# First attention: the triangular mask moves from TensorE's score sums to a selection by GpSimd on the exponentials

## The chip, the cores and the metric

The kernel runs on one core of one Trainium2 chip. The metric is the device time of the whole program in microseconds (us), lower is better. The kernel before takes 4102.77 us (median of three runs, 4102.47 to 4106.52).

## The reference, cut to what matters

Two transformer blocks run one after the other on x of shape 4 x 2048 x 256: an attention, a layer norm, a feed-forward part and a layer norm, twice. Both attentions have 16 heads of dimension 16 and are causal. The change is in the first one, whose score is a sum of three terms:

```python
scores = alpha * tanh(q @ k.T / beta)                 # per head
scores = scores + lam * hamming + lat                 # low-rank terms from x @ hex_w.T and x @ q6_w.T
scores = where(tril, scores, -inf)                    # keys after the query drop out
attn   = softmax(scores, axis=-1)
out    = attn @ v
```

Only the square blocks on the diagonal of the score matrix hold pairs on both sides of the triangle; blocks past it are never computed.

## The kernel before, in words

The program is a list of phases, one after the other: setup, projection of the first batch element, first attention (`attend_phase` with layer 0), a middle phase, second attention (layer 1), and a last phase. The change touches `attend_phase`, layer 0 only. The second attention masks in another way (VectorE takes the minimum with a table, `diagonal`) and is not altered.

**Tiling.** Scores are held transposed, keys on the 128 partitions and queries along the free axis. One *set* is one batch element and four heads; there are 16 sets. A set is a list of 34 *steps* (`even_steps`), 544 steps in all, each 128 partitions x (4 heads x 512 columns). The columns of a step are one key block against 512 queries, or two pieces of other widths. Ten steps of a set touch the diagonal. Steps 0, 7, 17 and 32 have one diagonal block of 128 columns for each head (512 elements per partition over the four heads); steps 1, 3, 8, 18, 20 and 33 have two (1024 elements per partition). Over 16 sets that is 64 and 96 steps.

**What each engine does for step S.** The engines run their own loops over S, tied by counting semaphores:

- TensorE, in iteration S of its loop and in this order: `weigh(S-2)` (probabilities of step S-2 times v, so LAG is 2), `extra(S,0)`, `extra(S,1)` (the low-rank score terms of heads 0 and 1), some background pieces, `scores(S+1, ...)` (q times k for the four heads of the next step, which waits for tanh of step S to have read its banks), `extra(S,2)`, more pieces, `extra(S,3)`. Each `extra` waits until VectorE has read the bank of two heads before.
- ScalarE alternates: tanh of step S (L929), then exp of step S-1 in place in `prob` (L940).
- VectorE, in `sums`, makes for each head alpha x tanh + extra into `prob` (L1004, four instructions of 128 x 512). Before the third of them it does one part of the normalisation of a finished group of queries, where one is due: a transpose (L971), a reciprocal (L974), a product (L978) or a transpose (L982).
- `prob` has R = 4 buffers; `sums(S)` waits for `weigh(S-4)`.

**The mask before.** In `extra`, for a piece on the diagonal, a second matmul (L866) adds a 128 x 128 table with -1e30 above the triangle to the bank. exp then gives zero there. `weigh(S)` waits for the count `pr`, that is, for exp of step S.

**Background.** While the first three batch elements are attended, the projections of the next one are made in the gaps: `pieces_at` on TensorE, `evict` on VectorE, and on GpSimd the split of each projected tile in three bf16 parts (L1033 to L1040, four instructions each for seven tiles per unit of 512 rows). This happens in sets 0 to 11; sets 12 to 15 have none, and there GpSimd has nothing at all to do. The plan gives pieces to TensorE in steps 9, 12 to 16, 19 and 24 to 31 of a set.

**Order.** SyncE issues loads three query groups ahead, stores of projected tiles and stores of results; all wait on counts of other engines. GpSimd issues no transfer.

Of the kernel before, what the change touches and what calls it, by code (L numbers as in the profile page):

```python
# [21 lines left out]
ALU = mybir.AluOpType  # L22
# [4 lines left out]
P = 128  # L27
# [5 lines left out]
CB = TG // P  # L33
HQ = 4
# [577 lines left out]
def attend_phase(nc, kn, layer, w=None):  # L612
# [7 lines left out]
    kept_at = [sum(1 for _, m in steps[:s] if m) for s in range(NST)]  # L620
    N_SET = B * NHQ
    N = N_SET * NST
    NG = N_SET * GB
    ND = sum(1 for _, m in steps if m)
    R = 4
    LAG = 2
    QU, KU = 3, 6
    QK0, E0, O0 = 0, 4, 6
# [3 lines left out]
    NU = len(kinds)  # L632
    NX = (B - 1) * GB if layer == 0 else 0
# [26 lines left out]
    with ExitStack() as ctx:  # L660
# [6 lines left out]
        sc = ph.count("sc")  # L667
        pr = ph.count("pr")
        kept = ph.count("kept")
        pv = ph.count("pv")  # L670
        o_tr, o_rc, o_mul, o_n = (ph.count(n) for n in ("o_tr", "o_rc", "o_mul", "o_n"))
# [5 lines left out]
        if layer == 0:  # L677
            f_s = ph.sb("f", [FR, QU, HQ, TG], BF16)
            g_s = ph.sb("g", [FR, KU, TG], BF16)
            tanh_s = ph.sb("tanh", [P, 2, HQ, TG])  # L680
        prob = ph.sb("prob", [P, R, HQ, TG])
# [4 lines left out]
        if layer == 0:  # L686
            w_in, x_in, ones_set = ph.sem("w_in"), [ph.sem(f"x_in{u}") for u in range(2)], ph.sem("ones_set")
            bg_ps, bg_ev = ph.count("bg_ps"), ph.count("bg_ev")
            hi, rest, mid, low = (ph.count(n) for n in ("hi", "rest", "mid", "low"))
# [9 lines left out]
        ps = kn["ps"]  # L699
        N_LOAD = NPART * (4 if layer == 0 else 2) + 2  # L700
        block = ctx.enter_context(nc.Block())

        def at(S):

            it, s = divmod(S, NST)
            return (it, s) + steps[s]
# [96 lines left out]
        def _(pe):  # L803
# [52 lines left out]
                    qk.done(mm)  # L856

            def extra(S, h):
                it, _, pieces, masked = at(S)

                sc.wait(pe, S * HQ + h - 2)
                for g, kb, q0, col, w in pieces:
                    n, c = it * GB + g, it * GB + kb // CB
                    mm = pe.matmul(ps[:, E0 + h % 2, col:col + w], g_s[:, c % KU, (kb % CB) * P:(kb % CB + 1) * P], f_s[:, n % QU, h, q0:q0 + w], start=True, stop=not masked)  # L864
                    if masked:
                        mm = pe.matmul(ps[:, E0 + h % 2, col:col + P], kn["identb"][:], kn["mask_kq"][:], start=False, stop=True)  # L866
                ex.done(mm)

            def weigh(S):
                it, s, pieces, masked = at(S)  # L870
                if layer == 0:
                    pr.wait(pe, S)
                elif masked:
                    kept.wait(pe, (it * ND + kept_at[s]) * 2 + 1)
                else:
                    pr.wait(pe, S * 2 + 1)
                for g, kb, q0, col, w in pieces:
                    n, c = it * GB + g, it * GB + kb // CB
                    if kb == 0:

                        o_tr.wait(pe, n - 2)
                        X = it - 1 if g == 0 else it
                        if g in ahead and 0 <= X < NX:

                            bg_ev.wait(pe, X * NU + ahead[g])
                    for h in range(HQ):
                        mm = pe.matmul(ps[VW * h:VW * (h + 1), O0 + n % 2, q0:q0 + w], v_s[:, c % KU, kb % CB, h * VW:(h + 1) * VW], prob[:, S % R, h, col:col + w], start=kb == 0, stop=g in ends[s] and (g, kb) == [p[:2] for p in pieces if p[0] == g][-1])  # L887
                pv.done(mm)
# [52 lines left out]

        @block.vector
        def _(dve):
            for c in (sc, o_tr, o_rc, o_mul, o_n, kept) + ((bg_ev,) if layer == 0 else ()):
                c.start(dve)
            dve.memset(oq_s[:], 0.0).then_inc(padded, 1)
            dve.wait_ge(padded, 1)
            if layer == 0:
                dve.memset(vs[:], 1.0).then_inc(ones_set, 1)
                dve.wait_ge(ones_set, 1)  # L950

            def evict(j):

                X, kind, m, tile, n, bank = unit(j)
                if kind == "v":
                    bg_ps.wait(dve, j)
                    v_out.wait(dve, m, X - 1)
                    bg_ev.done(dve.tensor_copy(vs[:, m, :, :, 0:HD], ps[:, bank].rearrange("p (t h d) -> p t h d", t=2, h=H)))
                elif kind != "g":
                    bg_ps.wait(dve, j)  # L960
                    low.wait(dve, tile - 2)
                    bg_ev.done(dve.tensor_copy(raw[0:n, tile % 2], ps[0:n, bank]))  # L962

            def normalise(due, count):

                for S, G, part in due[:count]:
                    v = G % 2
                    if part == 0:
                        pv.wait(dve, S)
                        o_mul.wait(dve, G - 2)  # L970
                        o_tr.done(dve.transpose(ot_s[:, v].rearrange("p b n -> p (b n)"), ps[:, O0 + v]))  # L971
                    elif part == 1:
                        o_tr.wait(dve, G)
                        o_rc.done(dve.reciprocal(rc_s[:, v], ot_s[:, v, :, HD]))  # L974
                    elif part == 2:
                        o_rc.wait(dve, G)
                        o_n.wait(dve, G - 2)
                        o_mul.done(dve.tensor_tensor(oq_s[:, v, :, 0:HD], ot_s[:, v, :, 0:HD], rc_s[:, v].unsqueeze(2).to_broadcast([P, NTB, HD]), ALU.mult))  # L978
                    else:
                        o_mul.wait(dve, G)  # L980
                        o_out.wait(dve, v, G // 2 - 1)
                        o_n.done(dve.transpose(on_s[:, v], oq_s[:, v].rearrange("p b n -> p (b n)")))  # L982
                del due[:count]

            def diagonal(S):

                masked = at(S)[3]
                for pair in range(2):
                    pr.wait(dve, S * 2 + pair)
                    block = blocks(prob[:, S % R, 2 * pair:2 * pair + 2], masked)  # L990
                    kept.done(dve.tensor_tensor(block, block, kn["keep"][:].unsqueeze(1).unsqueeze(1).to_broadcast([P, 2, len(masked), P]), ALU.min))  # L991

            def sums(S, due):

                pv.wait(dve, S - R)
                for h in range(HQ):
                    if h == 0 and unit_at(S) is not None:
                        evict(unit_at(S))
                    if h == 2:

                        normalise(due, 1)
                    th.wait(dve, S)
                    ex.wait(dve, S * HQ + h)
                    sc.done(dve.scalar_tensor_tensor(prob[:, S % R, h], tanh_s[:, S % 2, h], kn["alpha"][:, 0:1],  # L1004
                                                     ps[:, E0 + h % 2], ALU.mult, ALU.add))

            due = []
            for S in range(N + LAG + 1):
                if S > LAG:
                    it, s, *_ = at(S - LAG - 1)  # L1010
                    due += [(S - LAG - 1, it * GB + g, part) for g in ends[s] for part in range(4)]
                if S < N and layer == 0:
                    sums(S, due)
                else:
                    if S < N and at(S)[3]:
                        diagonal(S)
                    normalise(due, len(due))
            assert not due

        if layer == 0:  # L1020
            @block.gpsimd
            def _(pool):
                for c in (hi, rest, mid, low):
                    c.start(pool)
                for j in range(NX * NU):
                    X, kind, m, tile, n, bank = unit(j)
                    if kind == "v":
                        continue
                    u = tile % 2
                    src = f12[:, X % 2] if kind == "g" else raw[0:n, u]  # L1030
                    bg_ev.wait(pool, j)
                    parts_out.wait(pool, u, tile // 2 - 1)
                    hi.done(pool.tensor_copy(parts[0:n, u, 0], src))  # L1033
                    hi.wait(pool, tile)
                    low.wait(pool, tile - 1)
                    rest.done(pool.tensor_tensor(rem[0:n], src, parts[0:n, u, 0], ALU.subtract))
                    rest.wait(pool, tile)
                    mid.done(pool.tensor_copy(parts[0:n, u, 1], rem[0:n]))  # L1038
                    mid.wait(pool, tile)
                    low.done(pool.tensor_tensor(parts[0:n, u, 2], rem[0:n], parts[0:n, u, 1], ALU.subtract))  # L1040


def row_max_phase(nc, kn, layer, w=None):
# [990 lines left out]
```

## Time and profile before

| | |
|---|---|
| median of the runs | 4102.77 us |
| the profiled execution | 4100.62 us |
| its span, first to last instruction | 4098.8 us |
| mean granted TensorE clock | 0.97 |
| busy: TensorE / VectorE / ScalarE / GpSimd | 3696.2 / 2527.2 / 3502.5 / 623.6 us |
| first attention, first tanh to the end of the last exp | 133.5 to 2287.7 us |

Busy time says how long an engine had an instruction in work. Matmuls are pipelined, so that a busy TensorE is not one at its peak: the distance between the starts of successive instructions says what one of them costs, not its duration. Successive ScalarE instructions overlap by about 0.1 us in the same way.

### The profile page before, as it was taken

The numbers are of one execution on the slowest core, as the hardware profiler recorded it, in microseconds if no ns is written. First come the engines' busy times: TensorE is split into PE (matmuls) and PEld (weight loads), VectorE is DVE, ScalarE is ACT, GpSimd is POOL, SyncE is SP. The second block draws the span as 40 slices with busy tenths as digits, with TensorE's granted clock in tenths as the row PEclk, the third lists the DMA queues.
The fourth block names the chain that finished last, engine by engine and source line by source line (L and its number), as shares of the span: only waits on it lengthen the run. The fifth ranks groups of instructions, "written<-read, shape, count | busy, mean of one in ns | idle before, by whom it ended". The sixth has DMA issues, their size and how long they took to land. (4 is left out here: it accounts for less than half of the span.)

```text
span 4098.8 us, 62490 instructions
## 1 busy us (share of the span) xinstructions
PE 3696.2 (90%) x22198; PEld 1474.5 (36%) x22198; DVE 2527.2 (62%) x4349; ACT 3502.5 (85%) x2970; POOL 623.6 (15%) x659
## 2 busy tenths in 40 slices
PE   5699999999999999999989699969999999999798
PEld 2233333333333333333223366622222222222575
DVE  5577877787778777877788566732232323232576
ACT  2598999998999998999999566659999999999466
POOL 3112121211121112110000055510000000000232
PEclk9799999999999999999999899979999999999899
DMA  4322232222222322221121277642222222221331
GB/s 149 116 72 71 68 87 67 78 66 85 66 75 68 87 69 73 60 85 42 38 60 33 98 191 194 156 110 67 75 72 75 75 74 71 71 78 44 115 93 52
DMA packets 274745, 340.51 MB, mean 83 GB/s; under 512 B 40142, under 2 KB 207918, under 8 KB 274161
## 3 DMA queue, kind: packets, MB, share of 16 engines
q1 hardware_dynamic: 274420, 336.38, 28.1%
q8 instruction: 179, 2.93, 0.3%
q14 instruction: 146, 1.20, 0.1%
HBM read 207.97 MB, written 128.25 MB: 82 GB/s over the span
## 5 line engine op out<-in xcount | busy, mean ns | idle before, releaser
L1004 DVE SCALAR_TENSOR_TENSOR att_prob<-att_tanh,alpha,ps 128x512 f32<-128x512 f32 x2176 | 1513.9, 741 | 348.1 <-ACT att_tanh L929 189.7
L854 PE MATMUL ps<-att_q,att_k 99*128 99x512 bf16 (+5 forms) x5120 | 1138.5, 351 | 84.0 <-DMA att_v<-v_ones 61.2
L887 PE MATMUL ps<-att_prob,att_v 128*32 128x512 f32 (+3 forms) x10240 | 1173.3, 544 | 1.9 <-ACT att_prob L940 1.9
L929 ACT ACTIVATE att_tanh<-ps,rbeta 128x2048 f32<-128x2048 f32 x544 | 1083.4, 1992 | 73.6 <-PE ps L854 63.7
L940 ACT ACTIVATE att_prob<-att_prob 128x2048 f32<-128x2048 f32 x544 | 1053.2, 1936 | 91.7 <-DVE att_prob L1004 90.7
L935 ACT ACTIVATE att_prob<-ps 128x1024 f32<-128x1024 f32 x1088 | 1054.3, 1021 | 25.9 <-PE ps L854 9.8
L864 PE MATMUL ps<-att_f,att_g 75*128 75x512 bf16 (+3 forms) x2560 | 815.2, 357 | 159.4 <-DVE att_prob L1004 148.6
L854 PEld LDWEIGHTS ps<-att_q,att_k 96*128 96x128 bf16 (+1 forms) x5120 | 415.3, 98 | 897.2 <-ACT att_prob L935 427.3
L864 PEld LDWEIGHTS ps<-att_f,att_g 75*128 75x128 bf16 x2560 | 228.8, 97 | 942.9 <-DVE att_prob L1004 908.4
L991 DVE TENSOR_TENSOR att_prob<-att_prob,keep 128x512 f32<-128x512 f32 (+1 forms) x320 | 187.5, 586 | 580.6 <-ACT att_prob L935 579.5
L887 PEld LDWEIGHTS ps<-att_prob,att_v 128*32 128x32 f32 x10240 | 216.8, 108 | 367.1 <-issue 148.4
L1912 POOL TENSOR_SCALAR post_prev<-post_xt,post_om 128x512 f32<-128x512 f32 x64 | 56.8, 905 | 1233.0 <-issue 1124.6
L866 PE MATMUL ps<-mask_kq,identb 128*128 128x128 bf16 x1024 | 212.5, 221 | 0.0
L971 DVE STREAM_TRANSPOSE att_ot<-ps 128x512 f32<-128x512 f32 x128 | 91.2, 712 | 180.3 <-PE ps L887 180.3
L1683 POOL TENSOR_TENSOR mid_x1b<-mid_x,mid_bias 128x256 f32<-128x256 f32 x64 | 44.5, 729 | 626.2 <-ACT mid_x L1282 626.2
L1033 POOL CAST att_parts<-att_raw 128x512 bf16<-128x512 f32 (+1 forms) x72 | 43.8, 609 | 580.3 <-DVE att_raw L962 537.3
L1282 ACT ACTIVATE post_x<-post_rr,post_n_nb,post_n_rs 128x256 f32<-128x256 f32 x128 | 66.4, 589 | 65.6 <-DVE post_n_nb L1271 65.6
L1033 POOL CAST att_parts<-att_f 12x512 bf16<-12x512 f32 x12 | 7.2, 599 | 731.2 <-ACT att_f L922 731.2
L962 DVE COPY att_raw<-ps 128x512 f32<-128x512 f32 (+1 forms) x72 | 49.7, 690 | 98.0 <-PE ps L832 44.5
L1494 ACT ACTIVATE mid_parts<-mid_qcos 128x512 bf16<-128x512 f32 x64 | 40.1, 626 | 81.8 <-POOL mid_qcos L1657 81.6
L866 PEld LDWEIGHTS ps<-mask_kq,identb 128*128 128x128 bf16 x1024 | 101.2, 99 | 2.6 <-issue 0.7
L1040 POOL TENSOR_TENSOR att_parts<-att_rem,att_parts 128x512 bf16<-128x512 f32 (+2 forms) x84 | 97.1, 1156 | 15.1 <-POOL att_parts L1038 15.1
(162 smaller groups left out, 2975.7 us busy)
## 6 DMA issues: line engine op xcount, KB each, us to landing
att_v<-v_ones SPq DMA_DIRECT2D x128, 256.0 KB
att_k<-k_parts SPq DMA_DIRECT2D x128, 192.0 KB
att_q<-q_parts SPq DMA_DIRECT2D x128, 192.0 KB
att_k<-k_parts SPq DMA_DIRECT2D x128, 128.0 KB
att_q<-q_parts SPq DMA_DIRECT2D x128, 128.0 KB
o_t<-att_on SPq DMA_DIRECT2D x512, 32.0 KB, 1.8
v_ones<-mid_vs SPq DMA_DIRECT2D x64, 256.0 KB, 3.3
v_ones<-att_vs SPq DMA_DIRECT2D x96, 128.0 KB, 2.1
```

Source lines behind the costliest of these rows:

```text
L854: mm = pe.matmul(ps[:, bank, col:col + w], keys, q_s[:, n % QU, h, q0:q0 + w], start=True, stop=True)
L864: mm = pe.matmul(ps[:, E0 + h % 2, col:col + w], g_s[:, c % KU, (kb % CB) * P:(kb % CB + 1) * P], f_s[:, n % QU, h, q0:q0 + w], start=True ...
L866: mm = pe.matmul(ps[:, E0 + h % 2, col:col + P], kn["identb"][:], kn["mask_kq"][:], start=False, stop=True)
L887: mm = pe.matmul(ps[VW * h:VW * (h + 1), O0 + n % 2, q0:q0 + w], v_s[:, c % KU, kb % CB, h * VW:(h + 1) * VW], prob[:, S % R, h, col:col + ...
L929: th.done(act.activation(tanh_s[:, S % 2], ps[:, QK0:QK0 + HQ], ACT.Tanh, scale=kn["rbeta"][:, 0:1]))
L935: pr.done(act.activation(prob[:, S % R, 2 * pair:2 * pair + 2], ps[:, bank:bank + 2], ACT.Exp, scale=float(HD) ** -0.5))
L940: pr.done(act.activation(prob[:, (S - 1) % R], prob[:, (S - 1) % R], ACT.Exp))
L971: o_tr.done(dve.transpose(ot_s[:, v].rearrange("p b n -> p (b n)"), ps[:, O0 + v]))
L991: kept.done(dve.tensor_tensor(block, block, kn["keep"][:].unsqueeze(1).unsqueeze(1).to_broadcast([P, 2, len(masked), P]), ALU.min))
L1004: sc.done(dve.scalar_tensor_tensor(prob[:, S % R, h], tanh_s[:, S % 2, h], kn["alpha"][:, 0:1], ps[:, E0 + h % 2], ALU.mult, ALU.add))
L1040: low.done(pool.tensor_tensor(parts[0:n, u, 2], rem[0:n], parts[0:n, u, 1], ALU.subtract))
L1282: ins = act.activation(dst(t), src(t), ACT.Identity, scale=self.rs[:, u, t:t + 1], bias=self.nb[:, u, t:t + 1])
```

## The change

`extra` no longer issues the table's matmul (L866). Masked elements therefore go through tanh, sum and exp like all the others. On GpSimd a new function `hide(S)` waits for exp of step S (`pr`), and one `affine_select` in place writes zero where the key lies after the query, over the four heads and the one or two diagonal blocks of the step. It counts `kept`. `weigh(S)` of a masked step waits for `kept` in place of `pr`; the others wait for `pr` as before. GpSimd's loop now runs over the steps, with `hide(S-1)` ahead of the split of a tile that was finished in step S-1.

```diff
             def extra(S, h):
...
-                    mm = pe.matmul(ps[:, E0 + h % 2, col:col + w], g_s[...], f_s[...], start=True, stop=not masked)
-                    if masked:
-                        mm = pe.matmul(ps[:, E0 + h % 2, col:col + P], kn["identb"][:], kn["mask_kq"][:], start=False, stop=True)
+                    mm = pe.matmul(ps[:, E0 + h % 2, col:col + w], g_s[...], f_s[...], start=True, stop=True)
             def weigh(S):
                 it, s, pieces, masked = at(S)
-                if layer == 0:
+                if masked and layer == 0:
+                    kept.wait(pe, it * ND + kept_at[s])
+                elif layer == 0:
                     pr.wait(pe, S)
...
+                zero = pool.to_reg(0.0)
+                def hide(S):
+                    pr.wait(pool, S)
+                    block = blocks(prob[:, S % R], at(S)[3])
+                    kept.done(pool.affine_select(block, block, [[0, HQ], [0, len(at(S)[3])], [1, P]], ALU.is_ge, zero, base=0, channel_multiplier=-1))
...
+                for S in range(N + 1):
+                    if S > 0 and at(S - 1)[3]:
+                        hide(S - 1)
+                    if S > 0 and unit_at(S - 1) is not None:
+                        split(unit_at(S - 1))
```

## Rows read from the trace of the kernel before

**Rows 1.** Busy time by engine in two stretches: the first attention, set 12.

```profile
133.00:2288.00 2155.00, 1966.16 (x11974) 717.92 (x11976) 1688.59 (x2524) 2021.14 (x1100) 296.47 (x336) 0.98 0.23 68
...
1787.00:1911.00 124.00, 112.17 (x706) 36.25 (x704) 99.83 (x153) 124.00 (x69) 0.00 (x0) 1.00 0.17 51
```

**Rows 2.** Timeline, one plain iteration (set 14, step 16): start, duration, engine, line.

```profile
2092.45 2.01 ACT L940 ACTIVATE att_prob<-att_prob 128x2048 f32<-128x2048 f32 x1
...
2094.26 2.06 ACT L929 ACTIVATE att_tanh<-ps,rbeta 128x2048 f32<-128x2048 f32 x1
2094.54 0.16 PEld L887 LDWEIGHTS ps<-att_prob,att_v 128*32 128x32 f32 x8 [0.23 <-ACT att_prob L940]
...
2095.54 0.61 PE L864 MATMUL ps<-att_f,att_g 75*128 75x512 bf16 x2
...
2096.38 1.04 PE L854 MATMUL ps<-att_q,att_k 96*128 96x512 bf16 x4 [0.24 <-ACT att_tanh L929]
2096.41 2.73 DVE L1004 SCALAR_TENSOR_TENSOR att_prob<-att_tanh,alpha,ps 128x512 f32<-128x512 f32 x4 [0.92 <-ACT att_tanh L929]
...
2097.91 2.07 ACT L929 ACTIVATE att_tanh<-ps,rbeta 128x2048 f32<-128x2048 f32 x1
...
2099.76 2.02 ACT L940 ACTIVATE att_prob<-att_prob 128x2048 f32<-128x2048 f32 x1
```

**Rows 3.** Timeline of ScalarE, set 4: steps 20 and 32 and their successors.

```profile
765.41 1.97 ACT L929 ACTIVATE att_tanh<-ps,rbeta 128x2048 f32<-128x2048 f32 x1
...
769.48 1.95 ACT L929 ACTIVATE att_tanh<-ps,rbeta 128x2048 f32<-128x2048 f32 x1
...
815.26 1.97 ACT L929 ACTIVATE att_tanh<-ps,rbeta 128x2048 f32<-128x2048 f32 x1
...
819.63 1.95 ACT L929 ACTIVATE att_tanh<-ps,rbeta 128x2048 f32<-128x2048 f32 x1
```

**Rows 4.** Groups of instructions: the mask's matmuls (busy, mean ns | idle).

```profile
L866 PE MATMUL ps<-mask_kq,identb 128*128 128x128 bf16 x1024 | 212.5, 221 | 0.0
```

**Rows 5.** Timeline of TensorE in set 4: one of them, and its successor.

```profile
767.98 0.22 PE L866 MATMUL ps<-mask_kq,identb 128*128 128x128 bf16 x1
768.04 0.27 PE L864 MATMUL ps<-att_f,att_g 75*128 75x256 bf16 x1
```

**Rows 6.** Groups of instructions on GpSimd, in three phases (busy, mean ns | idle).

```profile
L1657 POOL TENSOR_TENSOR mid_qcos<-mid_qcos,mid_qsin 128x512 f32<-128x512 f32 x64 | 80.8, 1274 | 108.5 <-DVE mid_qsin L1583 108.3 <-issue 0.2
...
L1912 POOL TENSOR_SCALAR post_prev<-post_xt,post_om 128x512 f32<-128x512 f32 x64 | 56.8, 905 | 1233.0 <-issue 1124.6 <-ACT post_xt L1839 108.4
...
L1033 POOL CAST att_parts<-att_raw 128x512 bf16<-128x512 f32 (+1 forms) x72 | 43.8, 609 | 580.3 <-DVE att_raw L962 537.3 <-DMA k_parts<-att_parts 43.1
```

**Rows 7.** Timeline: ScalarE hands over to GpSimd, and GpSimd to ScalarE.

```profile
453.42 0.57 ACT L922 ACTIVATE att_f<-ps 12x512 f32<-12x512 f32 x1
...
454.25 0.60 POOL L1033 CAST att_parts<-att_f 12x512 bf16<-12x512 f32 x1 [60.67 <-ACT att_f L922]
...
2439.87 0.63 ACT L1494 ACTIVATE mid_parts<-mid_qcos 128x512 bf16<-128x512 f32 x1 [0.17 <-POOL mid_qcos L1657]
```

**Rows 8.** Timeline, an iteration with a transpose (set 13, step 14).

```profile
1964.76 1.41 DVE L1004 SCALAR_TENSOR_TENSOR att_prob<-att_tanh,alpha,ps 128x512 f32<-128x512 f32 x2 [0.60 <-ACT att_tanh L929]
...
1966.09 0.70 DVE L982 STREAM_TRANSPOSE att_on<-att_oq 128x512 f32<-128x512 f32 x1
...
1966.71 1.36 DVE L1004 SCALAR_TENSOR_TENSOR att_prob<-att_tanh,alpha,ps 128x512 f32<-128x512 f32 x2
...
1968.11 2.02 ACT L940 ACTIVATE att_prob<-att_prob 128x2048 f32<-128x2048 f32 x1
```

**Rows 9.** The product L978: its durations (minimum/median/maximum ns), and one beside GpSimd.

```profile
L978 DVE TENSOR_TENSOR att_oq<-att_ot,att_rc x128: 416/424/1362, 173.7 to 3798.4; 128x256 f32<-128x256 f32 x128
...
468.05 1.16 POOL L1036 TENSOR_TENSOR att_rem<-att_raw,att_parts 128x512 f32<-128x512 f32 x1 [0.28 <-POOL att_parts L1033]
...
468.13 1.36 DVE L978 TENSOR_TENSOR att_oq<-att_ot,att_rc 128x256 f32<-128x256 f32 x1
```

More of the change, by code:

```diff
@@ L858, in extra @@
             def extra(S, h):
-                it, _, pieces, masked = at(S)
+                it, _, pieces, _ = at(S)
                 sc.wait(pe, S * HQ + h - 2)
@@ L863, in extra @@
                     n, c = it * GB + g, it * GB + kb // CB
-                    mm = pe.matmul(ps[:, E0 + h % 2, col:col + w], g_s[:, c % KU, (kb % CB) * P:(kb % CB + 1) * P], f_s[:, n % QU, h, q0:q0 + w], start=True, stop=not masked)
-                    if masked:
-                        mm = pe.matmul(ps[:, E0 + h % 2, col:col + P], kn["identb"][:], kn["mask_kq"][:], start=False, stop=True)
+                    mm = pe.matmul(ps[:, E0 + h % 2, col:col + w], g_s[:, c % KU, (kb % CB) * P:(kb % CB + 1) * P], f_s[:, n % QU, h, q0:q0 + w], start=True, stop=True)
                 ex.done(mm)
@@ L943, in _ @@
         def _(dve):
-            for c in (sc, o_tr, o_rc, o_mul, o_n, kept) + ((bg_ev,) if layer == 0 else ()):
+            for c in (sc, o_tr, o_rc, o_mul, o_n) + ((bg_ev,) if layer == 0 else (kept,)):
                 c.start(dve)
@@ L1022, in _, with split @@
             def _(pool):
-                for c in (hi, rest, mid, low):
+                for c in (hi, rest, mid, low, kept):
                     c.start(pool)
-                for j in range(NX * NU):
+                zero = pool.to_reg(0.0)
[3 more added lines that the diff above has]
+                    kept.done(pool.affine_select(block, block, [[0, HQ], [0, len(at(S)[3])], [1, P]], ALU.is_ge, zero, base=0, channel_multiplier=-1))
+                def split(j):
                     X, kind, m, tile, n, bank = unit(j)
                     if kind == "v":
-                        continue
+                        return
                     u = tile % 2
```

## The prediction

> **What bounds the kernel now.** I read the busy time by stretch first. In the first attention (2155 us) ScalarE is busy 2021 us, TensorE 1966; in set 12, where no projections run beside it, ScalarE is busy 124.00 of 124.00 us and GpSimd does nothing [rows 1]. So the stage runs at ScalarE's pace. The timeline then gives the period: tanh starts at 2094.26 and again at 2097.91, so a step costs 3.65 us (tanh plus exp) [rows 2]. 544 steps x 3.65 = 1986 us; the rest of the stage is steps in which something reaches ScalarE late. The question is what is late after the change, and by how much; TensorE's busy share says nothing here.
>
> I put the plain iteration on a clock that starts with tanh(S) at 0 [rows 2]: exp(S-2) ends at 2094.46, that is 0.20; weigh(S-2) starts at 0.28; the first two extras start at 1.28; scores(S+1) run from 2.12 (they wait for the end of tanh(S)) to 3.16; tanh(S+1) starts at 3.65. VectorE's four sums run from 2.15 to 4.88, exp(S) starts at 5.50. weigh(S-2) starts 0.08 after the exp that it needs: it has no spare time of its own, only what lies behind it on TensorE has.
>
> **What goes.** 1024 mask matmuls, 212.5 us of busy time [rows 4]. But the next matmul starts 0.06 us after the mask's [rows 5], so what TensorE gets back is 1024 x 0.06 = 61 us, and only where TensorE is what ScalarE waits for is it worth anything. In set 4 two masked steps are longer than 3.65: step 20 (765.41 to 769.48, 4.07) and step 32 (815.26 to 819.63, 4.37) [rows 3]. In the 12 sets with projections this is at most 12 x (0.42 + 0.72) = 14 us; both have background pieces around them. Up to four masks stand ahead of the scores (0.24 us); step 20 is followed by a select's wait anyway, so I count 2 us.
>
> **What comes.** 160 selections, 64 of 512 and 96 of 1024 elements per partition, each between exp(S-2) and weigh(S-2). The trace has no selection. GpSimd's one-input rows for 512 elements take 0.61 us (cast) and 0.905 us (two constants, f32 to f32); two inputs take 1.274 us [rows 6]. Lower bound: 1024 elements at the price of a 1.5-fold cast, D = 0.9 (D1 = 0.6 for 512); upper: twice the two-input row, D = 2.55 (D1 = 1.27). The nearest row is the two-constant one, as a selection also computes a value, compares and writes f32: D1 = 0.9 and twice that, D = 1.8. Handing over costs too: ScalarE's instruction ends at 453.99 and GpSimd's starts at 454.25, 0.26 us; out of GpSimd 0.17 us are seen towards ScalarE [rows 7], 0.15 towards TensorE is my estimate. So weigh(S-2) starts at w = 0.20 + 0.26 + D + 0.15 = D + 0.61 in place of 0.28.
>
> The Trainium skill (GPSIMD Engine Reference, section 3.1) gives about 1.8 cycles per element at best for a tight loop at 1.2 GHz, 0.77 us for 512 elements; estimated from that page D would be 1.54 and, by the sum below, the time about 4203 us. The 0.905 us row of this trace is slower than that rule.
>
> **What is late then.** Queued behind weigh on TensorE are the extras, the scores and the last extras; ScalarE waits for the scores, VectorE for the extras, ScalarE for VectorE. Without masks the scores start 1.0 + 0.44 after w at the earliest and end at w + 2.48; with 0.04 to hand over, tanh(S+1) is late by w + 2.52 - 3.65 = **D - 0.52**. VectorE's first sum follows the first extra by 0.53 (estimate: 0.39 us matmul and a handover), ends at w + 1.53 + 2.73, so exp(S) is late by w + 4.30 - 5.50 = D - 0.59: less. But with a normalising transpose before the third sum VectorE takes 3.31 us (1964.76 to 1968.07) and exp follows after 0.04, at 5.50: no spare time there [rows 8]. Then exp(S) is late by w + 4.88 - 5.50 = **D**. With a reciprocal (0.25) it is D - 0.3.
>
> The iterations that wait for a selection are S = M + 2 for masked step M. A transpose is due in iterations 2, 5 and 9 of a set (groups of queries end in steps 3, 8, 20 and 33, the four parts fall due from three steps later), that is for M = 0, 3 and 7; a reciprocal in iteration 3, for M = 1. Two masked steps in a row share: the second exp is done on time while tanh was held, so the second selection starts early by what the first one cost, and the pair costs what the second alone would, or the first if more. Per set, with D = 1.8:
> - M = 3: D = 1.80
> - M = 7, 8: larger of D1 = 0.9 and D - 0.52 = 1.28
> - M = 17, 18: 1.28; M = 20: 1.28; M = 32, 33: 1.28
> - M = 0, 1 (next set): D - 0.3 = 1.50
>
> Sum 8.42 us, or 6D - 2.4; x 16 sets = 135 us. In the 12 sets with projections TensorE is late for other reasons in some of these iterations (step 20 by 0.42 [rows 3]), and a selection hides behind that; I take twice that, 0.84 us per set, 10 us, off. Take off 2 us for the masks, add 2 for the last selection, with nothing behind it. **+125 us.**
>
> Other edits cost nothing: GpSimd's splits run in the same order, and a split takes four instructions of 0.6 to 1.2 us within a step or so of its eviction; each masked step after one is over a step away. GpSimd issues no transfer, and no queue is passed. The second attention is untouched.
>
> The profiled execution took 4100.62 us (span 4098.8), 2.15 less than the median; 4100.6 + 125 = 4225.6, and beside the median **4228 us**.
>
> **The rivals.**
> - *The selection is longer than any GpSimd row suggests*, D over 2.55. For: it computes an index per element, and no row does. Against: all 512-element rows lie between 0.6 and 1.3. At D = 2.55 the sum is 16 x 12.9 = 206, less 10: 4299 us. At D = 3.5, 16 x 18.6 - 10 = 288: 4391 us.
> - *VectorE's product and the selection block each other.* L978 takes 0.42 us, but 1.36 beside a GpSimd instruction that ends at 469.21; it ends at 469.49 [rows 9]: it waited for it. The sums do not show this, and the product is due in iterations 4, 8, 13 and 25, about 3.5 after tanh, while selections start 0.46 after tanh in iteration M + 2. In iterations 4 and 8 (next to M = 3 and 7) they miss each other by some 0.1 us. If they meet: up to 2 per set x 16 x 1.4 us (1.8 less 0.4 spare) = 45 us: 4273 us. The Trainium skill (SBUF — State Buffer, SBUF: two separate sides) calls the shared pair of ports an exclusive lock, held for a whole instruction, for a VectorE instruction with two SBUF inputs. The trace agrees, with this row.
> - *Not slower*: the selection fits in what TensorE has spare, and the masks' 14 us come back. Place: the wait of weigh. It decides at D = 0.52 for plain iterations, while M = 3, 7 and 0 cost D or D1 whatever it is; with D = 0.2 and D1 = 0.1 it is 16 x 0.4 = 6 us against up to 14: 4103 - 8 = 4095 us. Against: no row for 512 elements is under 0.6 us.
> - *The spare time is larger than I read*, the lower bound of D with pairs fully shared: D = 0.9, 16 x 3.3 - 10 = 43 us: 4146 us. This is the low edge of the forecast, not another mechanism.
>
> **How the numbers follow.** Forecast with D from 0.9 to 2.55: 0.80. Longer selection: 0.10. Blocking with VectorE: 0.05. Not slower: 0.05, of which 0.02 is faster by over 0.2% (8 us, about what a measurement can tell from no change) and 0.03 within. Slower: 0.95. The range takes the forecast's own bounds, 4146 and 4299, and a little of the longer selection: 4145 to 4310 us.
>
> **What would show it.** The L866 group is gone; a GpSimd group of 160 selections stands at about 0.9 us (64) and 1.8 us (96). The wait of weigh's weight loads on GpSimd is 160 times some 2 us. Tanh starts in iterations 2, 5 and 9 to 10, 19 to 20, 22, 0 to 1 and 3 come 3.65 plus the stalls above; all others keep 3.65; the second attention keeps its length. ScalarE stays at 3.65 us of work per step and is idle some 125 us more. I am wrong in size if the selection is not 1.8 us, in mechanism if it is and the stalls per set are not 6D - 2.4, or if steps that wait for no selection become longer.

## The result, and the profile after

The changed kernel takes 4171.0 us (median of four runs, 4166.9 to 4179.2) against 4103.9 us: ratio 1.0168, 95% interval 1.0156 to 1.0180, 67 us slower. It was forecast slower, 4228 us with a range of 4145 to 4310: the direction and the main mechanism hold, the amount is about half of the 125 us forecast.

The profiled execution took 4169.7 us, 69.1 more than that of before. From the first tanh of the first attention to the last, it is 2216.5 us and was 2147.2: all 69 us are in this stage. First the busy time by engine, in the whole stage and in set 13 (no projections); they answer to [rows 1]. Each such row has the stretch and its length, the busy time (and count of instructions) of TensorE, its weight loads, VectorE, ScalarE and GpSimd, then the granted clock as a share of 2.4 GHz, the DMA share and GB/s.

```profile
133.00:2357.00 2224.00, 1925.25 (x10943) 660.94 (x10940) 1680.35 (x2524) 2035.40 (x1100) 443.76 (x495) 0.97 0.22 66
1967.90:2095.80 127.90, 107.68 (x642) 32.96 (x641) 100.61 (x154) 126.44 (x70) 9.98 (x11) 1.00 0.17 50
```

ScalarE is no longer busy all the time in a set without projections (126.44 of 127.90). Then the selection, by group and by its spread (minimum/median/maximum ns), and who waited for it. The mask's matmuls [rows 4] are gone.

```profile
L1032 POOL TENSOR_SCALAR_AFFINE_SELECT att_prob<-att_prob 128x1024 f32<-128x1024 f32 (+1 forms) x160 | 148.8, 930 | 1327.0 <-ACT att_prob L940 1294.2
...
L1032 POOL TENSOR_SCALAR_AFFINE_SELECT att_prob<-att_prob x160: 652/1098/1111, 141.9 to 2357.4; 128x1024 f32<-128x1024 f32 x96, 128x512 f32<-128x512 f32 x64
...
PEld ps L887 <- POOL att_prob L1032: 137.8, 134, 3.2
PE ps L887 <- POOL att_prob L1032: 99.3, 116, 2.3
```

The timeline of iteration 3 of set 13, which waits for the selection of step 1 (two blocks); it answers to [rows 2]. As in the prediction, w is the start of weigh, counted from the start of that iteration's tanh.

```profile
1977.40 1.90 ACT L940 ACTIVATE att_prob<-att_prob 128x2048 f32<-128x2048 f32 x1
1979.20 1.96 ACT L929 ACTIVATE att_tanh<-ps,rbeta 128x2048 f32<-128x2048 f32 x1
1979.46 1.10 POOL L1032 TENSOR_SCALAR_AFFINE_SELECT att_prob<-att_prob 128x1024 f32<-128x1024 f32 x1 [3.27 <-ACT att_prob L940]
1980.62 0.38 PEld L887 LDWEIGHTS ps<-att_prob,att_v 128*32 128x32 f32 x16 [1.20 <-POOL att_prob L1032]
...
1981.62 0.61 PE L864 MATMUL ps<-att_f,att_g 75*128 75x256 bf16 x4
...
1982.07 1.03 PE L854 MATMUL ps<-att_q,att_k 96*128 96x512 bf16 x4
...
1983.14 1.97 ACT L929 ACTIVATE att_tanh<-ps,rbeta 128x2048 f32<-128x2048 f32 x1
```

exp ends at 1979.30, the selection starts 0.16 later, takes 1.10 and ends at 1980.56, weigh follows 0.06 later: w is 1.42. The scores end at 1983.10, and the next tanh comes 3.94 after the last in place of 3.65. The forecast's relation w + 2.52 - 3.65 gives 0.29, and 0.29 it is. With one block (here iteration 9 of set 14) the selection takes 0.68 us and w is 1.00:

```profile
2130.66 1.96 ACT L929 ACTIVATE att_tanh<-ps,rbeta 128x2048 f32<-128x2048 f32 x1
...
2130.93 0.68 POOL L1032 TENSOR_SCALAR_AFFINE_SELECT att_prob<-att_prob 128x512 f32<-128x512 f32 x1 [14.32 <-ACT att_prob L940]
2131.66 0.16 PEld L887 LDWEIGHTS ps<-att_prob,att_v 128*32 128x32 f32 x8 [1.03 <-POOL att_prob L1032]
```

Iteration 5 of set 13, with a normalising transpose on VectorE; it answers to [rows 8].

```profile
1986.81 1.95 ACT L929 ACTIVATE att_tanh<-ps,rbeta 128x2048 f32<-128x2048 f32 x1
...
1989.75 1.41 DVE L1004 SCALAR_TENSOR_TENSOR att_prob<-att_tanh,alpha,ps 128x512 f32<-128x512 f32 x2 [1.23 <-PE ps L864]
...
1991.07 0.71 DVE L982 STREAM_TRANSPOSE att_on<-att_oq 128x512 f32<-128x512 f32 x1
...
1993.10 1.91 ACT L940 ACTIVATE att_prob<-att_prob 128x2048 f32<-128x2048 f32 x1 [0.40 <-DVE att_prob L1004]
```

exp starts 6.29 after tanh, not 5.50: late by 0.79; w + 4.88 - 5.50 gives 0.80.

I took the starts of all 544 tanh from both timelines and compared them step by step. Regular differences, the same in nearly every set (us per set):

```
iteration    waits for        by the forecast's formula   measured, sets
             selection of     at w = 1.42 or 1.00         with projections / without
1            33 (32 before)   0.29                        0.28 / 0.34
3            1  (0 before)    0.50 (reciprocal)           0.28 / 0.24
5 and 6      3                0.80 (transpose)            0.80 / 0.79
9 and 10     7, 8             0.38 (transpose)            0.65 / 0.38
19 and 20    17, 18           0.29                        0.58 / 0.32
22           20               0.29                        0.28 / 0.28
24           none (cause open) -                          0.18 / 0.13
sum                           2.55                        3.05 / 2.5
```

Iteration 2 waits for a selection too (step 0) and has a normalising transpose, but is no later than before (0.02): iteration 1 just ahead of it had already been held.

12 x 3.05 + 4 x 2.5 = 47 us. Beside them stand 12 iterations, in steps 3, 9, 19 and 22 of some sets, that are another 1.5 to 2.1 us longer, some 19 us in all. The last 4 us are spread over other steps. One of the 12 (set 14, step 3), and the granted clock over it and over its sibling in set 13 (the column behind POOL's):

```profile
2106.33 1.10 POOL L1032 TENSOR_SCALAR_AFFINE_SELECT att_prob<-att_prob 128x1024 f32<-128x1024 f32 x1 [3.27 <-ACT att_prob L940]
...
2107.48 1.93 PE L887 MATMUL ps<-att_prob,att_v 128*32 128x128 f32 x16 [0.90 <-POOL att_prob L1032]
...
2109.35 1.03 PE L864 MATMUL ps<-att_f,att_g 75*128 75x256 bf16 x4
...
2111.59 1.97 ACT L929 ACTIVATE att_tanh<-ps,rbeta 128x2048 f32<-128x2048 f32 x1 [1.60 <-PE ps L854]
...
2106.00:2112.00 6.00, 4.91 (x33) 2.11 (x37) 3.73 (x8) 4.34 (x4) 1.10 (x1) 0.72 0.38 117
1979.00:1985.00 6.00, 4.56 (x39) 1.63 (x38) 4.99 (x9) 5.93 (x4) 1.10 (x1) 1.00 0.42 133
```

The selection and weigh's start are the same as in set 13; then weigh takes 1.93 us and not 1.07. The granted clock is 1.00 (2.4 GHz) from 2106.07 to 2107.40, while TensorE waits, and 0.50 (1.2 GHz) from 2107.50 to 2110.80, from weigh's start on; over the 6 us that is 0.72. Set 13 has the same wait and keeps its clock. In all 12 the clock falls between 0.9 and 1.9 us after tanh, about where weigh starts (1.00 or 1.42).

### The profile page after: what moved, and what is told of

Its sections match the earlier page's. It is cut to its first block and busy times, and to the rows that moved or that the text cites. A ratio compares the mean times of both kernels' runs of the same rounds, so it can differ in the third digit from the quotient of the medians.

```text
span 4167.9 us, 60763 instructions
## 1 busy us (share of the span) xinstructions
PE 3654.7 (88%) x21174; PEld 1418.7 (34%) x21174; DVE 2517.8 (60%) x4349; ACT 3516.7 (84%) x2970; POOL 771.8 (19%) x819
## 5 line engine op out<-in xcount | busy, mean ns | idle before, releaser
L929 ACT ACTIVATE att_tanh<-ps,rbeta 128x2048 f32<-128x2048 f32 x544 | 1068.3, 1964 | 115.2 <-PE ps L854 106.8
L940 ACT ACTIVATE att_prob<-att_prob 128x2048 f32<-128x2048 f32 x544 | 1038.0, 1908 | 104.5 <-DVE att_prob L1004 100.7
L864 PE MATMUL ps<-att_f,att_g 75*128 75x512 bf16 (+3 forms) x2560 | 785.4, 361 | 171.2 <-DVE att_prob L1004 170.5
L854 PEld LDWEIGHTS ps<-att_q,att_k 96*128 96x128 bf16 (+1 forms) x5120 | 428.2, 98 | 894.7 <-ACT att_prob L935 425.9
L864 PEld LDWEIGHTS ps<-att_f,att_g 75*128 75x128 bf16 x2560 | 201.9, 97 | 957.0 <-DVE att_prob L1004 883.0
L1032 POOL TENSOR_SCALAR_AFFINE_SELECT att_prob<-att_prob 128x1024 f32<-128x1024 f32 (+1 forms) x160 | 148.8, 930 | 1327.0 <-ACT att_prob L940 1294.2
L1673 POOL TENSOR_TENSOR mid_qcos<-mid_qcos,mid_qsin 128x512 f32<-128x512 f32 x64 | 80.8, 1274 | 108.6 <-DVE mid_qsin L1599 108.4
L1050 POOL TENSOR_TENSOR att_parts<-att_rem,att_parts 128x512 bf16<-128x512 f32 (+2 forms) x84 | 97.1, 1156 | 15.1 <-POOL att_parts L1048 15.1
L982 DVE STREAM_TRANSPOSE att_on<-att_oq 128x512 f32<-128x512 f32 x128 | 90.6, 707 | 2.2
L1598 DVE TENSOR_TENSOR mid_qcos<-ps,mid_cos 128x512 f32<-128x512 f32 x64 | 44.0, 687 | 72.6 <-PE ps L1436 71.5
```

The costliest lines, as they stand in the source:

```text
L854: mm = pe.matmul(ps[:, bank, col:col + w], keys, q_s[:, n % QU, h, q0:q0 + w], start=True, stop=True)
L929: th.done(act.activation(tanh_s[:, S % 2], ps[:, QK0:QK0 + HQ], ACT.Tanh, scale=kn["rbeta"][:, 0:1]))
L940: pr.done(act.activation(prob[:, (S - 1) % R], prob[:, (S - 1) % R], ACT.Exp))
L1032: kept.done(pool.affine_select(block, block, [[0, HQ], [0, len(at(S)[3])], [1, P]], ALU.is_ge, zero, base=0, channel_multiplier=-1))
```

## The experiments

Two questions: is the wait the whole loss, and where do the iterations at the lower clock come from? No mask, aside, both masks (first time) and later ran together on one chip (kernel before there: 4102.9 us), twice, fill, between and LAG 3 on a second (4102.9), and the changed kernel again, both masks again and the last two LAG 3 kernels on a third (4103.5). Each ratio is to the kernel before on the same chip. The edits are against the changed kernel unless it says otherwise.

**No mask.** In `weigh` and GpSimd's loop:

```diff
-                if masked and layer == 0:
-                    kept.wait(pe, it * ND + kept_at[s])
-                elif layer == 0:
+                if layer == 0:
                     pr.wait(pe, S)
...
-                    if S > 0 and at(S - 1)[3]:
-                        hide(S - 1)
```

> Leaves out the triangular mask of the first attention altogether: no mask matmuls, no selection, weigh waits for exp. Theory (the selection's latency ahead of weigh is the whole loss, and the masks' matmuls were hidden behind ScalarE): before minus 0 to 5 us, some 4100 us. Rival (the matmuls taken away were worth what stands before them in steps 20 and 32, 14 us, so that the selection cost 80 and not 67 us): 4090 us.

Measured: 4101.3 us against 4102.9, ratio 0.9996 (0.9987 to 1.0005). Against before only step 20 changed regularly: 0.24 us or more shorter in the sets with projections, 4 us in all; step 32 kept its 4.36. So 212 us of busy matmuls were worth at most some 4 us in the profile, and no more than the noise in the medians (1.6 us, the interval holds 1); the selection with its wait costs about 70 and not 80.

**Selection aside.**

```diff
+            scr_s = ph.sb("scr", [P, HQ, 2, P])
...
+                if layer == 0:                  # weigh
                     pr.wait(pe, S)
...
+                if S >= R and at(S - R)[3]:     # sums
+                    kept.wait(dve, o_it * ND + kept_at[o_s])
...
+                    kept.wait(pool, it * ND + kept_at[s] - 1)
-                    kept.done(pool.affine_select(block, block, ...))
+                    kept.done(pool.affine_select(scr_s[:, :, 0:len(at(S)[3])], block, ...))
```

> The 160 selections are made, but into a scratch tile that nobody reads; weigh waits for exp only, so the mask is left out of the result. VectorE waits for the selection of four steps earlier before it overwrites what was read, which has long ended. Theory (only the wait costs): the same as without any mask, within 3 us, some 4100 us. Rival (GpSimd's reads of SBUF hold up VectorE or its own splits): 4115 us or more, with L978 or L1043 late.

Measured: 4101.8 us, ratio 0.9995 (0.9986 to 1.0004), the same as without any mask. The selections are all there and as long as before:

```profile
L1036 POOL TENSOR_SCALAR_AFFINE_SELECT att_scr<-att_prob x160: 651/1098/1109, 141.7 to 2289.5; 128x1024 f32<-128x1024 f32 x96, 128x512 f32<-128x512 f32 x64
```

GpSimd's work, its traffic in SBUF and its place ahead of the splits cost nothing that these medians show; only that weigh waits for it does. This rules out the rival in which the selection and VectorE's product block each other: of the 128 products L978, 22 take some 1.36 us in the changed kernel, 24 in this one, and 23 did before, beside GpSimd's splits [rows 9].

**Both masks**, run twice.

```diff
-                    ... start=True, stop=True)
+                    ... start=True, stop=not masked)
+                    if masked:
+                        mm = pe.matmul(ps[:, E0 + h % 2, col:col + P], kn["identb"][:], kn["mask_kq"][:], start=False, stop=True)
```

> The mask matmuls are put back, the selection and its wait stay. Theory: where TensorE is late because of the selection, in iterations 1, 3 and 20 of a set, the up to four mask matmuls ahead of the scores (0.06 us each) now stand on the path: 3 x 0.24 x 16 = 11 us more than the changed kernel, some 4182 us. Rival (the masks' matmuls keep TensorE busier and its clock up, so that the slow stretches go): 4155 us.

> Selection and mask matmuls together once more, on the same chip as the changed kernel. Theory (the mask matmuls cost 6 to 11 us on the path in iterations 1, 3 and 20, and take away slow stretches of TensorE in iterations 9, 19 and 22 by keeping it busy in the masked steps ahead): 8 to 18 us less than the changed kernel on the same chip. Rival (the 15 us between them were the chance of two chips): the same, or up to 11 us more.

Measured: 4156.0 us (four runs, ratio 1.0124) the first time, 4165.1 (4152.8 to 4168.0, ratio 1.0143) the second. The changed kernel beside the second:

> The changed kernel once more, unaltered, for a comparison with more runs. Theory: 4165 to 4180 us as before.

Measured: 4171.2 us (4164.1 to 4182.4), ratio 1.0173. So more work on TensorE made the kernel faster, here by 6 us in the medians and 12 by the ratios (15 us across chips), though single runs of the two overlap. That is so although iterations 1 and 3 became 0.24 us longer each in nearly every set, as expected. My first expectation, 11 us more, was wrong by its sign.

What is gained is the clock, but for the most part not behind a selection. In steps 9 and 19 the two profiles of the changed kernel have 15 iterations of 64 with the clock down (12 in step 9, 3 in step 19), the two with both masks none. In steps 3, 5 and 22 nothing is gained: 7 iterations with the clock down in the changed kernel (2, 0 and 5), 10 with both masks (3, 5 and 2). By the starts of tanh the gain in steps 9, 19 and 22 is about eaten up by what iterations 1, 3, 5 and 20 lose. The stage is 15.1 and 9.8 us shorter in the two pairs of profiles, and steps 27 and 28, where no masked step stands near, are shorter by 13.0 and 11.2 us of it (the clock is down there in 7 and 8 sets of the changed kernel, 4 and 6 with both masks). Those two steps also change from set to set in the kernel before (last section), so the masks are not shown to be the cause there.

Windows over steps 8 and 9 of set 6 in the changed kernel, then in the kernel with both masks, second time (TensorE's busy time is the first number behind the length):

```profile
1016.90:1020.60 3.70, 3.21 (x21) 1.06 (x20) 2.85 (x6) 3.70 (x3) 0.00 (x0) 1.00 0.37 117
1020.60:1026.80 6.20, 5.45 (x19) 0.81 (x17) 3.48 (x6) 3.80 (x4) 1.78 (x2) 0.72 0.33 95
```

```profile
1021.50:1025.20 3.70, 3.63 (x29) 1.45 (x29) 2.85 (x6) 3.70 (x3) 0.00 (x0) 1.00 0.41 122
1025.20:1029.80 4.60, 3.97 (x21) 0.87 (x19) 3.49 (x6) 3.79 (x4) 1.35 (x2) 1.00 0.45 129
```

Step 8 has two diagonal blocks. With masks TensorE is busy 3.63 us of it, without 3.21; then both wait the same for the selection of step 7, and only the changed kernel loses its clock. That is not enough to tell when it falls: in its other profile the changed kernel has the same set 6 with the same 3.21 us and the clock at 1.00 in both steps.

**Fill.**

```diff
+                if layer == 0 and LAG <= S < N and (S - LAG) % NST in (1, 3, 7, 17, 20, 32):
+                    sc.wait(pe, S * HQ - 2)
+                    for _ in range(3):
+                        (the matmuls of extra(S, 0), without its count)
                 if S >= LAG:
                     weigh(S - LAG)
```

> As the changed kernel, but ahead of weigh of masked steps 1, 3, 7, 17, 20 and 32 TensorE repeats the matmuls of the coming first extra three times, into the same bank, as soon as VectorE has left it; the result is the same. Theory (a dozen iterations in which TensorE falls to 1.2 GHz after it idled ahead of weigh cost 1.5 us each; the fill keeps it busy, and ends before the selection does): no iteration of 5.2 us or more in steps 3, 9, 19 and 22, and 15 to 20 us less than the changed kernel, 4152 us. Rival (the slow iterations have nothing to do with TensorE's idle time): 4171 us or more, with the slow iterations still there.

Measured: 4184.8 us, ratio 1.0211: slower than the changed kernel. The fill waits for VectorE's third sum, and in iterations 3, 5 and 9 that came so late that the fill ended after the selection: weigh started up to 2.27, 1.86 and 1.60 after tanh and not 1.42, 1.41 and 1.00 (in iterations 19 and 0 it was 1.36). In iteration 22 the fill fits, weigh starts at 1.42 as before in the 12 sets with projections, and none of 16 sets has the clock down there, against three and two in the profiles of the changed kernel; in step 19 none against three and none, in step 9 one against four and eight. But in step 3 the clock is down in six sets, against two and none, though TensorE was given more to do there. So the theory is neither shown nor refuted by the counts; as a time the experiment failed.

**Twice.**

```diff
+                    dup.wait(pool, it * ND + kept_at[s] - 1)
                     pr.wait(pool, S)
...
+                    dup.done(pool.affine_select(scr_s[...], block, ...))
                     kept.done(pool.affine_select(block, block, ...))
```

> Each selection is made twice, first into a scratch tile, then in place, so that weigh of a masked step can start at 2.5 (two blocks) or 1.7 (one) after tanh and not at 1.42 or 1.0. Theory (a stall is what is left when weigh's start is held against the spare time on TensorE and VectorE, and two masked steps in a row share it): 9.1 us per set and not 2.5 to 3.1, so 145 us over before without slow stretches of TensorE, with them 4250 to 4270 us. Rival (each selection costs its own duration on the path): 149 us on top of the changed kernel, 4320 us.

Measured: 4341.8 us (4329 to 4344), 239 over before, outside both expectations. Where the clock stayed up the relation holds (w is 2.47 with two blocks): iteration 22 of sets 4 and 8 is 1.33 us late, iterations 19 and 20 of sets 12 and 14 together 1.39; expected 1.39 for both. But in most late iterations the clock now falls too: 3.5 us in iterations 3 and 22 in many sets. Windows over the stage (all but its last 55 us), and over iteration 9 of set 4:

```profile
133.00:2475.00 2342.00, 2002.75 (x10708) 680.99 (x10707) 1647.72 (x2465) 1988.72 (x1073) 581.62 (x650) 0.91 0.21 62
788.70:796.90 8.20, 6.82 (x19) 1.03 (x17) 3.48 (x6) 3.77 (x3) 3.46 (x4) 0.58 0.28 81
```

A doubled wait costs more than double: over the waits by the relation (145 us) stand some 94 us more, and beside them the mean granted clock of the stage falls from 0.97 to 0.91. The block between GpSimd and VectorE is seen here too, but small: six of the products L978 take 0.70 us, beside a selection.

**Weigh later**, behind both extras, and **between** them.

```diff
                 if S >= LAG and not held:       # held: step S - LAG is masked
                     weigh(S - LAG)
                 if layer == 0 and S < N:
                     extra(S, 0)
+                    if held: weigh(S - LAG)     # "between"
                     extra(S, 1)
+                    if held: weigh(S - LAG)     # "later"
```

> As the changed kernel, but TensorE issues weigh of a masked step behind the first two extras and not ahead of them. Theory: weigh can then start at about 1.5 after tanh (the second extra waits for VectorE until 1.25), the scores end at 3.55, in time for tanh at 3.65; the stalls of 0.28 to 0.8 us per iteration go, and with them the long idle time of TensorE and its slow stretches: 4100 to 4108 us. Rival (the loss is not the place of the wait in TensorE's order but the selection's latency anywhere): 4150 us or more.

> Weigh of a masked step stands between the first and the second extra. The first can run at 0.6 after tanh while the selection is under way, weigh at 1.42, the scores end at 3.7. Theory (each instruction group moved ahead of weigh helps if it is ready by then; the second extra was not, it waits for VectorE's last sum at 1.25 and later): stalls of 0.1 us in place of 0.28 to 0.8, 4115 to 4135 us. Rival (anything ahead of weigh makes VectorE's chain later, as with both extras ahead): 4171 us or more.

Measured: later 4196.7 us (1.0224), between 4132.7 (1.0064; 1.0050 to 1.0078). The first expectation was wrong by nearly 100 us. The second extra of iterations 0 and 1 of set 13, weigh, the scores and the next tanh in the kernel "later":

```profile
2003.76 0.39 PE L864 MATMUL ps<-att_f,att_g 75*128 75x512 bf16 x1 [0.27 <-DVE att_prob L1007]
2004.08 0.16 PEld L887 LDWEIGHTS ps<-att_prob,att_v 128*32 128x32 f32 x8 [0.23 <-issue]
...
2007.91 0.39 PE L864 MATMUL ps<-att_f,att_g 75*128 75x128 bf16 x2 [0.27 <-DVE att_prob L1007]
...
2008.23 0.38 PEld L887 LDWEIGHTS ps<-att_prob,att_v 128*32 128x32 f32 x16 [0.21 <-issue]
...
2009.24 1.04 PE L854 MATMUL ps<-att_q,att_k 96*128 96x512 bf16 x4
...
2010.31 1.97 ACT L932 ACTIVATE att_tanh<-ps,rbeta 128x2048 f32<-128x2048 f32 x1 [0.38 <-PE ps L854]
```

Weigh waits for no selection any more ("issue"), but the second extra waits for VectorE, whose sums wait for the extras of the iteration before: 1.33 after tanh in iteration 0, 1.75 in iteration 1, and weigh's 1.0 us now stands behind that wait, where before it filled it. Only the first extra was free to move: with it alone ahead, the stalls are 0.07 in iterations 1, 2, 5 and 22 and 0.09 in iteration 19, though iterations 3, 9 and 20 keep 0.2 to 0.6 in most sets, and iterations at the lower clock stay in steps 5, 9 and 20 (2, 9 and 5 of 16).

**LAG 3.**

```diff
-    LAG = 2
+    LAG = 3 if layer == 0 else 2
-    plan = ["9a 9b", "12a 12b 12b 13a", ..., "24a 24b 24b 25a", ...]
+    plan = ["9a 9b", "12b 12b 12b 13a", ..., "24b 24b 24b 25a", ...]
```

> LAG is 3 in the first attention: TensorE weighs step S-3 in iteration S, whose exp and selection ended a step earlier; the units that start in steps 12 and 24 put their first piece behind the third extra, because the transpose that frees their bank comes one step later. Theory (the loss is the selection's latency in a place where TensorE had 0.08 us to spare): weigh never waits for GpSimd, the stalls and the slow stretches go, 4095 to 4106 us. Rival (something else that the selection brings costs the time): 4140 us or more.

Measured: 4094.2 us (median of 11 runs, 4093.3 to 4102.2), ratio 0.9981 (0.9972 to 0.9990): 1 us under the range expected, and some 9 us faster than the kernel before. Iteration 5 of set 13, and the stage:

```profile
1928.67 2.05 ACT L929 ACTIVATE att_tanh<-ps,rbeta 128x2048 f32<-128x2048 f32 x1
1928.93 0.16 PEld L887 LDWEIGHTS ps<-att_prob,att_v 128*32 128x32 f32 x8 [0.23 <-ACT att_prob L940]
...
1929.02 1.10 POOL L1032 TENSOR_SCALAR_AFFINE_SELECT att_prob<-att_prob 128x1024 f32<-128x1024 f32 x1 [6.21 <-ACT att_prob L940]
...
1932.32 2.06 ACT L929 ACTIVATE att_tanh<-ps,rbeta 128x2048 f32<-128x2048 f32 x1
...
133.00:2288.00 2155.00, 1906.27 (x10952) 647.52 (x10954) 1657.04 (x2524) 2020.59 (x1100) 444.77 (x496) 0.99 0.23 68
```

The selection still takes 1.10 us, beside weigh of the step before, which doesn't wait for it; the period is 3.65. None of the products L978 takes 1.36 us any more (they fall due a step later); what that is worth is not shown. The four `prob` buffers that were there are enough.

**LAG 3 with the table**, in the kernel before, and **LAG 3 with a moved plan** (`"12b 13a 13b 14a"`, `"14b 15a 15b 16a"`, `"16b 17a 17b 19a"`, `"24b 25a 25b 26a"`, and the last four units half to one step later).

> The kernel before (mask in TensorE, no selection) with LAG 3 and the two moved pieces. Theory (with LAG 3 the selection costs nothing, and the masks' matmuls are worth 0.24 us in step 20 of the 12 sets with projections and nothing elsewhere): 3 to 5 us more than LAG 3 with the selection, 4097 to 4100 us. Rival (the selection still costs, and LAG 3 alone is what gained): less than with the selection, 4085 us.

> LAG 3 with the selection, and the background plan moved one half to one step later as a whole in place of bunching three pieces behind the third extra of steps 12 and 24. Theory (the bunched pieces cost some 16 us net in steps 11 to 16, 25 and 26): 4075 to 4085 us. Rival (the moved plan brings TensorE's slow stretch in steps 27 and 28 back, as in the kernel before, 4 us a time): 4090 to 4105 us.

Measured: table 4112.2 us (median of 12, but 4089.7 to 4138.3; ratio 1.0026, 1.0003 to 1.0049), moved plan 4100.5 (0.9996; 0.9988 to 1.0005). Both medians are outside what I expected. The reasoning for the table agrees in the profile: its stage is 2138.9 us with the clock never down in steps 27 and 28; that of LAG 3 with the selection is 2145.0, but with the clock down there in three sets, at 3.7 us each. Without them it would be 2134, 5 us less than with the table, as forecast for the matmuls. But by medians, on two chips, the table is 18 us slower, and more spread than any kernel here. Its one kept profile is of a run of 4095.5 us, so what half of its runs lose stays open, and with it whether the selection beats the table at LAG 3. The moved plan did not bring its 15 us; 4100.5 is in the rival's range, but not by the rival's cause: in its profile the clock is down in steps 27 and 28 of one set only, and the moved pieces make steps 28 to 33 longer, by 15 us in all against before.

## Why the prediction was right

- *What bounds, and the clock of an iteration*: right. With w as measured, w + 2.52 - 3.65 gave the stall of iteration 22 (in sets with projections also that of 1 and 3) and w + 4.88 - 5.50 that of iterations 5 and 6 (in sets without projections also that of 9 and 10) to 0.01 us; in sets without projections iterations 1, 3 and 19 to 20 are within 0.05. The sharing between two masked steps holds (iterations 19 and 20 together 0.32 in sets without projections).
- *What the masks give back*: forecast 2 us; the profile without masks shows some 4, in step 20 alone, and the medians 1.6, not clear of noise.
- *The selection's duration* was the term that was mis-sized: D = 1.80 for two blocks and 0.90 for one, measured 1.10 and 0.68, nearer the cast's row [rows 6] than the two-constant row that I took as nearest, and under the estimate of 1.54 for two blocks as well. Doubling a row of 512 elements also doubles what it costs to start: from 0.68 and 1.10 a selection is 0.26 us and 0.82 ns per element.
- *Handing over*: forecast 0.26 + 0.15, measured 0.16 + 0.06. The 0.17 that I read as GpSimd's handover to ScalarE [rows 7] is ScalarE's idle time; GpSimd's sum ends at 2439.77 (2438.49 + 1.28), 0.10 before ScalarE starts. Besides, exp ends 0.10 rather than 0.20 behind the start of tanh in these iterations. Together w is 1.42, forecast 2.41; it is D + 0.32, not D + 0.61. This also answers the prediction's own sign of a wrong mechanism, stalls per set other than 6D - 2.4: at D = 1.1 that is 4.2 us and 2.5 to 3.05 were measured, but 0.29 less in each of six terms is 1.7 us, and 2.5 is left. Its other sign, a longer step that waits for no selection, did appear: iteration 24, by 0.13 to 0.18 us.
- *The reciprocal in iteration 3*: forecast 0.2 more than the plain case, measured nothing; why is open.
- *Sets with projections*: I took 0.84 us per set off. It is the other way: iterations 9 and 19 pay 0.65 and 0.30 where, without projections, 9 and 10 pay 0.38 and 19 nothing: 0.55 per set more. That fits a TensorE that is already late and has no spare time left; no run takes the pieces away to show it.
- *TensorE's clock* was not in the sum: 12 iterations at the lower clock, 19 us in the profile. Without it the terms as measured give 47, not 67. With D = 1.1 my own sum, 16 x (6 x 1.1 - 2.4) = 67 us less 10, would have said 57 (59 with 0.68 for the one block of M = 7): near 67, but by errors that offset each other. So the time lay in the range by the width given to D, and partly by luck.
- The rival of a long selection is out (1.10 us), so is the blocking of L978 by the selection (22 long ones, 23 before), and so is "not slower".

By the Trainium skill (TensorE: Matmul & The Clock Gate, HAM oscillation) waits that recur between bursts of matmuls can put the clock back again and again. The trace agrees: 0.72 over iteration 3 of set 14 and, with the doubled wait, 0.58 over iteration 9 of set 4. That section's case is one of long waits for transfers; here TensorE had waited 0.90 us for the selection when the clock fell, and after the same wait it stayed up in most sets of that profile. What decides it is not shown.

## What to carry to other kernels

Work taken off an engine that is not the bound bought nothing clear here, while a step put between a producer and a consumer that starts 0.1 us behind it costs its whole latency less the spare time behind the consumer; ask for that spare time first, branch by branch. If an extra stage is wanted there, let the consumer run one step later (a larger lag, if the buffers allow it) and not elsewhere within its step: what stood at the old place may have been filling another wait. And a short wait on TensorE can cost twice, once as time and once as clock: look at the granted clock right behind it.

## What was not expected of the hardware

The selection over 128 x 1024 f32 took 1.10 us on GpSimd, less than its sum of two inputs over 128 x 512 (1.27). And nearly all kernels, that of before too, have iterations that come at one of two speeds: steps 27 and 28 of a set, where TensorE is the bound, take 9.4 us together or 13.1 to 13.4. In the kernel before, set 6 and set 7 (the clock is the column behind POOL's):

```profile
1067.65:1081.00 13.35, 12.86 (x41) 3.96 (x42) 7.90 (x12) 7.76 (x4) 7.04 (x8) 0.62 0.30 85
1206.80:1216.20 9.40, 8.38 (x41) 3.10 (x42) 7.68 (x12) 7.76 (x4) 5.63 (x7) 1.00 0.31 89
```

Seven of twelve sets had the clock down there before, seven and eight in the two profiles of the changed kernel, three with LAG 3, none with LAG 3 and the table. In LAG 3's profile the stage is 2 us shorter than before: step 20 gives 4 us and steps 27 and 28 give 12, the bunched pieces lose some 18, and the start of the first set gives 2. But that profile is of the slowest of its 11 runs (4102.2 us, the median is 4094.2), so where the 9 us of the medians come from is not shown. Which set falls is not settled here.
